# Three mask banks and one rank bank in the fuse stage, with the second rank piece of a row block issued behind the step's sums

## The chip, the cores and the metric

The kernel runs on one core of one Trainium2 chip. The metric is device time in microseconds (us); lower is better. The engines are TensorE (PE; its weight loads are listed as PEld), VectorE (DVE), ScalarE (ACT), GpSimd (POOL) and SyncE (SP), which issues the transfers. Each engine works through its own instructions in program order and waits on semaphores for the others. PE writes only into PSUM, whose eight banks of 128 x 512 fp32 are all in use in the stage that is changed.

## What is computed

Eight graphs of 1024 nodes with 128 features pass through four residual layers: an attention layer, a graph network on a thinned adjacency, a normalised-adjacency convolution and a max-degree layer. The second one is what matters here:

```python
def step(carry, n):                      # _dilate_pattern, one row after the other
    row = jnp.take(carry, n, axis=0)
    nbi = row.astype(jnp.int32)
    num = jnp.sum(nbi)
    sf = jnp.where(num > T_DIL, (num + K_DIL - 1) // K_DIL, 1)
    rank = jnp.cumsum(nbi)
    rm = row & (rank % sf == 0)
    ...
    keep = ~rm
    carry = carry.at[n].set(row & keep)
    carry = carry.at[:, n].set(carry[:, n] & keep)
...
adj_d = adj * keep
deg = jnp.clip(jnp.sum(adj_d, axis=-1, keepdims=True), 1.0, None)
agg = jnp.einsum('bij,bjd->bid', adj_d, x) / deg
out = agg @ Wr + x @ Wx + b
out = out / jnp.maximum(norm(out), NORM_EPS)
```

## The kernel before

The program is a row of stages: `attention_phase`, `removal_phase` (which settles how many entries each row loses), `fuse_phase`, two `layer_phase`s, `gcn_phase` and `maxdeg_phase`. The change lies in `fuse_phase` alone. It works on one graph `b` after the other, 0 to 7. For each graph it masks the transposed adjacency with the entries that were removed and adds up the first sage layer over it. At the same time it works out, for graph `b + 1`, which entries of each row were removed ("low").

A graph has eight row blocks of 128 rows, and the loop takes one block, a step `st`, at a time. What PE issues in a step, in this order:

- `masks(b, st, 0)` and `masks(b, st, 1)`: the two halves of the block's mask, 512 columns each, in one of the NM mask banks `pmask`. DVE's `masked_rows` (L1241) multiplies the adjacency by each half and then raises `masked`, which frees the bank. PE waits for this at L1060 before it writes mask number n, until mask n - NM is done.
- `ranks(b + 1, st)`: running counts along the rows of the next graph, in one of the NR rank banks `prank`. Blocks 0 to 3 have one piece of at most 512 columns, blocks 4 to 7 a first piece of 512 columns and a second one of 128 to 512, so a graph has 12 pieces. ACT's `distances` (L1162) reads each piece into a `dist` buffer in SBUF and raises `dist_ready`, which frees the bank. DVE's `removals` (L1229) compares it, which gives `low`, and frees the dist buffer. PE waits for `dist_ready` before it writes piece n, until piece n - NR has been read.
- side work in the one bank `misc`, by `misc_uses`: a product or a set of transposes in each step (`z` in step 0 and 7, `o2` in 1 and 2, `turn_r` in 3 and 4, `turn_h` in 5 and 6), which ACT, or DVE for `o2`, copies out before the next use.
- `sums(b, st - 1)`: eight fp32 products of the masked rows of the step before (L1113), added up in the three banks `acc`. `sums(b, 7)` comes behind step 7.

ACT works in each step through `distances(b + 1, st)` for all pieces of the block, then the side copy. Behind it come `squares(b - 1)` in step 0, `rectified(b - 1)` (L1190) in step 1, `norm_root` in step 2 and `norm_apply` (L122, eight instructions) in step 3. DVE works through `masked_rows(b, st)`, then `outputs(b - 1)` in step 0, `removals(b + 1, st)`, `projected` (L1247) for `o2` in steps 1 and 2, `weights` in step 1, `norm_mean` in step 2, `norm_scale` in step 3 and `batch_statistics` in step 6.

Ahead of the loop there is a prologue for graph 0: all its rank pieces, with `turn_h` and the first `z` between the first ones. PE may begin the masks of a graph once all 12 pieces of `low` for it are there (`low_ready`). Graph 7 has no next graph, so it runs without ranks.

Of the kernel before, what the change touches and what calls it, by code (L numbers as in the profile page):

```python
# [7 lines left out]
ACT = mybir.ActivationFunctionType  # L8
F32 = mybir.dt.float32
BF16 = mybir.dt.bfloat16  # L10
F16 = mybir.dt.float16
# [5 lines left out]
P = 128  # L17
HALF = 512
# [930 lines left out]
def fuse_phase(nc, z, A, K, scratch):  # L949

    B, N, NB, NH, HB, D = z.B, z.N, z.NB, z.NH, z.HB, z.D
    pieces = [(nb, hf * HALF, min((hf + 1) * HALF, (nb + 1) * P)) for nb in range(NB) for hf in range(NH)
              if hf * HALF < (nb + 1) * P]
    low0 = [sum((i + 1) * P for i in range(j)) for j in range(NB + 1)]
    NR, NM = 2, 2
    NC, CB = NB // 2, 2
    NP, NW = len(pieces), NB * NH
    ZW, AW = D + 1, 170
# [1 line left out]
    adjT = K["adj"]  # L960
    with Scope(nc, "fuse") as s:
        low = s.sb("low", [P, low0[NB]], BF16)
        dist = [s.sb(f"dist{i}", [P, HALF], F16) for i in range(NR)]
        h = K["h"]
        hT = s.sb("hT", [P, N], F32)
        zz = s.sb("z", [P, NB, ZW], F32)
# [5 lines left out]
        prank = [s.ps(f"prank{i}", [P, HALF]) for i in range(NR)]  # L972
# [15 lines left out]
        def of_block(nb):  # L988
            return [q for q in range(NP) if pieces[q][0] == nb]
# [22 lines left out]
        with nc.Block() as block:  # L1012
# [25 lines left out]
            @block.tensor  # L1038
            def _(pe):
                t = nc.tensor  # L1040

                def ranks(b, nb):

                    for q in of_block(nb):
                        _, lo, hi = pieces[q]
                        n = b * NP + q
                        if n >= NR:
                            pe.wait_ge(dist_ready, n - NR + 1)
                        first_jb, last_jb = lo // P, min(nb, (hi - 1) // P)
                        for jb in range(first_jb, last_jb + 1):  # L1050
                            a = max(jb * P, lo)
                            mm = t.matmul(prank[n % NR][:, a - lo:hi - lo], T8[:, b, jb, nb * P:(nb + 1) * P],  # L1052
                                          K["fore8"][:, a - jb * P:hi - jb * P], start=(jb == first_jb), stop=(jb == last_jb))
                        mm.then_inc(rank_ready, 1)

                def masks(b, pb, hf):

                    n = b * NW + pb * NH + hf
                    if n >= NM:
                        pe.wait_ge(masked, n - NM + 1)  # L1060
                    o = pmask[n % NM]
                    c0 = hf * HALF
                    own, up = (pb + 1) * P - c0, max(0, pb * P - c0)
                    if up < HALF:
                        t.matmul(o[:, up:HALF], K["minus8"][:], T8[:, b, pb, c0 + up:c0 + HALF], start=True, stop=False)
                    for c, k in ((0, min(HALF, up)), (up, P if 0 < own <= HALF else 0)):
                        if k > 0:
                            t.matmul(o[:, c:c + k], K["ident16"][:], low[:, low0[pb] + c0 + c:low0[pb] + c0 + c + k],
                                     start=(up >= HALF), stop=False)
                    for e in range(HB):  # L1070
                        qb = hf * HB + e
                        piece = o[:, e * P:(e + 1) * P]
                        if qb >= pb:
                            mm = t.matmul(piece, low[:, low0[qb] + pb * P:low0[qb] + (pb + 1) * P], K["ident16"][:],  # L1074
                                          start=False, stop=(e == HB - 1))
                        else:
                            mm = t.matmul(piece, T8[:, b, pb, qb * P:(qb + 1) * P], K["minus8"][:],
                                          start=False, stop=(e == HB - 1))
                    mm.then_inc(mask_ready, 1)

                def side_work(kind, b, half):

                    n = use_number[(kind, b, half)]
                    if n > 0:
                        pe.wait_ge(misc_free, n)
                    if kind == "turn_h":
                        if b > 0:
                            pe.wait_ge(h_ready, b)
                    elif kind == "turn_r":
                        pe.wait_ge(r_ready, b * 2 + half + 1)  # L1090
                    else:
                        pe.wait_ge(hT_ready, b * 2 + half + 1)
                    for e in range(HB):
                        ib = half * HB + e
                        if kind == "turn_h":
                            mm = t.transpose(miscv[:, e, :], h[:, ib, :], K["ident"][:])
                        elif kind == "turn_r":
                            mm = t.transpose(miscv[:, e, :], o[b % 2][:, ib, :], K["ident"][:])
                        else:
                            mm = t.matmul(miscv[:, e, :], hT[:, ib * P:(ib + 1) * P], K["Wr0" if kind == "z" else "Wx0"][:],  # L1100
                                          start=True, stop=True)
                    mm.then_inc(misc_ready, 1)

                def sums(b, jb):

                    if jb == 0 and b == 0:
                        pe.wait_ge(ones_ready, 1)
                    pe.wait_ge(z_ready, b * 2 + jb // HB + 1)
                    pe.wait_ge(masked, b * NW + (jb + 1) * NH)
                    for ib in range(NB):  # L1110
                        if jb == 0 and b > 0 and ib % 3 == 0:
                            pe.wait_ge(acc_free, 3 * (b - 1) + ib // 3 + 1)
                        mm = t.matmul(acc_tile(ib)[:, 0:ZW], adjT[b % 2][:, jb, ib * P:(ib + 1) * P], zz[:, jb, :],  # L1113
                                      start=(jb == 0 and ib % 3 == 0), stop=(jb == NB - 1), skip_group_check=True)
                    mm.then_inc(added, 1)
                    if jb == NB - 1:
                        pe.drain().then_inc(sums_ready, 1)

                ranks(0, 0)
                side_work("turn_h", 0, 0)  # L1120
                ranks(0, 1)
                side_work("turn_h", 0, 1)
                ranks(0, 2)
                ranks(0, 3)
                side_work("z", 0, 0)
                for nb in range(4, NB):
                    ranks(0, nb)
                for b in range(B + 1):
                    if b < B:
                        pe.wait_ge(low_ready, (b + 1) * NP)  # L1130
                    if b == B:
                        keep_busy(t, K, pmask[0][:], 26)
                    for st in range(NB):
                        if b < B:
                            for hf in range(NH):
                                masks(b, st, hf)
                            if b + 1 < B:
                                ranks(b + 1, st)
                        for use in misc_uses(b, st):
                            side_work(*use)  # L1140
                        if b < B and st > 0:
                            sums(b, st - 1)
                    if b < B:
                        sums(b, NB - 1)

            @block.scalar
            def _(act):
                a = nc.scalar
# [4 lines left out]
                def distances(b, nb):  # L1153
                    for q in of_block(nb):
                        _, lo, hi = pieces[q]
                        n = b * NP + q
                        act.wait_ge(rank_ready, n + 1)
                        if n >= NR:
                            act.wait_ge(dist_done, n - NR + 1)
                        tile = b * NB + nb  # L1160
                        bias = K["kb"][:, tile:tile + 1] if lo == 0 else K["kbhigh"][:, nb - NB // 2, b:b + 1]
                        a.activation(dist[n % NR][:, 0:hi - lo], prank[n % NR][:, 0:hi - lo], ACT.Abs, bias=bias)  # L1162
                        act.drain().then_inc(dist_ready, 1)  # L1163

                def side_copy(kind, b, half):
# [55 lines left out]
            def _(dve):  # L1221
                v = nc.vector

                def removals(b, nb):
                    for q in of_block(nb):
                        _, lo, hi = pieces[q]
                        n, tile = b * NP + q, b * NB + nb
                        dve.wait_ge(dist_ready, n + 1)
                        v.tensor_scalar(low[:, low0[nb] + lo:low0[nb] + hi], dist[n % NR][:, 0:hi - lo],  # L1229
                                        K["kd"][:, tile:tile + 1], None, ALU.is_equal).then_inc(low_ready, 1)  # L1230
                        dve.drain().then_inc(dist_done, 1)

# [893 lines left out]
```

## Time and profile before

| | |
|---|---|
| median of 3 runs | 1295.79 us (1294.36 to 1296.54) |
| profiled execution | 1293.96 us, span of its instructions 1292.2 us |
| PE, weight loads, DVE, ACT busy | 1156.5, 934.5, 780.2, 589.5 us |
| fuse stage | from 342.4 to about 643 us of the span |

The span runs from the first to the last instruction; the time of the execution also has what lies around it. Starts of rows in a timeline are counted from the start of the span. Matmuls are pipelined, so a row's length is longer than the distance to the next start. The distance between starts is therefore what a group of matmuls costs where nothing waits.

### The profile page before, as it was taken

To read this page: it belongs to the slowest core of one execution; us is meant where nothing else is said; L and a number is where in the kernel's file an instruction comes from. 1 tells how busy PE (TensorE), PEld (TensorE's weight loads), DVE (VectorE), ACT (ScalarE), POOL (GpSimd) and SP (SyncE) were. 2 spreads that over 40 slices of the span, in tenths; PEclk is the share of its full clock that TensorE was granted. 3 is DMA by queue.
4 is the path that set the end of the run, shared out by engine and by line. 5 is a ranking of instruction groups with operands and counts; after the bars stand their busy time and mean duration, and the time that the engine had idled before them with its cause. 6 is when DMAs were issued, how large, how long until landed. Compare 5 with 4: busy or idle time off the path is not lost. (4 is left out here: it accounts for less than half of the span.)

```text
span 1292.2 us, 27195 instructions
## 1 busy us (share of the span) xinstructions
PE 1156.5 (89%) x9833; PEld 934.5 (72%) x9833; DVE 780.2 (60%) x2899; ACT 589.5 (46%) x1533; POOL 114.7 (9%) x129
## 2 busy tenths in 40 slices
PE   4999698887598898898989999899999899997998
PEld 4999666664387777777879999699999655553554
DVE  5998577776556665656634453543536455545983
ACT  4888456566645544445222434413343443323441
POOL 3442000000000000000000000022323020110000
PEclk9999888876699999999989999999999899998999
DMA  8967012110335566555316575036757336543921
GB/s 327 327 262 284 11 24 34 23 27 14 135 129 231 228 250 240 225 190 205 133 49 260 230 281 224 22 123 232 289 208 303 131 131 256 218 177 128 407 68 49
DMA packets 105514, 228.93 MB, mean 177 GB/s; under 512 B 34528, under 2 KB 53152, under 8 KB 105376
## 3 DMA queue, kind: packets, MB, share of 16 engines
q1 hardware_dynamic: 104656, 227.07, 47.2%
q8 instruction: 81, 1.33, 0.4%
q14 instruction: 57, 0.47, 0.1%
q10 hardware_dynamic: 720, 0.07, 0.0%
HBM read 185.70 MB, written 37.75 MB: 173 GB/s over the span
## 5 line engine op out<-in xcount | busy, mean ns | idle before, releaser
L1431 PE MATMUL lay_acc<-lay_z,k_otheradj 128*128 128x128 f32 x1024 | 118.3, 277 | 0.0
L1431 PEld LDWEIGHTS lay_acc<-lay_z,k_otheradj 128*128 128x128 f32 x1024 | 117.1, 194 | 0.0
L1431 PE MATMUL lay_acc<-lay_z,k_keepadj 128*128 128x128 f32 x1024 | 117.0, 275 | 0.0
L1431 PEld LDWEIGHTS lay_acc<-lay_z,k_keepadj 128*128 128x128 f32 x1024 | 115.6, 192 | 0.0
L1479 ACT ACTIVATE lay_junk<-lay_o 128x128 bf16<-128x128 f32 x128 | 37.8, 296 | 124.7 <-DVEq L1568 124.5
L1545 DVE TENSOR_TENSOR lay_o<-lay_ring,k_vec 128x512 f32<-128x512 f32 x32 | 22.1, 692 | 108.1 <-PE lay_ring L1424 108.1
L1525 POOL TENSOR_TENSOR lay_bl<-k_vec,k_mask 128x256 f32<-128x256 f32 x32 | 21.2, 663 | 607.1 <-DVEq L1558 603.4
L333 PE MATMUL att_acc<-att_rhs,att_adjT 128*128 128x130 f32 x512 | 60.0, 281 | 13.3 <-POOLq L285 12.3
L333 PEld LDWEIGHTS att_acc<-att_rhs,att_adjT 128*128 128x128 f32 x512 | 59.3, 196 | 13.9 <-POOLq L285 12.4
L1162 ACT ACTIVATE fuse_dist<-fuse_prank,k_kb 128x512 f16<-128x512 f32 (+2 forms) x64 | 38.4, 600 | 60.7 <-PE fuse_prank L1052 59.3
L1113 PE MATMUL fuse_acc<-fuse_z,k_otheradj 128*128 128x129 f32 x512 | 63.5, 277 | 0.9 <-DVEq L1263 0.8
L1487 ACT ACTIVATE lay_o<-lay_o,lay_nrm 128x128 f32<-128x128 f32 x128 | 39.4, 389 | 54.2 <-DVE lay_nrm L1579 54.2
L1113 PE MATMUL fuse_acc<-fuse_z,k_keepadj 128*128 128x129 f32 x512 | 63.1, 277 | 0.8 <-DVEq L1263 0.8
L1241 DVE SCALAR_TENSOR_TENSOR k_otheradj<-fuse_pmask,k_otheradj 128x512 f32<-128x512 f32 x64 | 44.1, 689 | 28.9 <-PE fuse_pmask L1074 16.4
L1113 PEld LDWEIGHTS fuse_acc<-fuse_z,k_otheradj 128*128 128x128 f32 x512 | 59.9, 192 | 2.0 <-DVEq L1263 1.6
L1113 PEld LDWEIGHTS fuse_acc<-fuse_z,k_keepadj 128*128 128x128 f32 x512 | 59.8, 192 | 1.7 <-DVEq L1263 1.2
L1229 DVE TENSOR_SCALAR fuse_low<-fuse_dist,k_kd 128x512 bf16<-128x512 f16 (+2 forms) x96 | 30.7, 320 | 49.7 <-ACTq L1163 44.8
L333 PE MATMUL att_acc<-att_rhs,k_keepadj 128*128 128x130 f32 x512 | 58.1, 276 | 1.8 <-DVEq L441 0.9
L333 PEld LDWEIGHTS att_acc<-att_rhs,k_keepadj 128*128 128x128 f32 x512 | 57.5, 191 | 2.4 <-issue 2.4
L1052 PE MATMUL fuse_prank<-k_fore,k_T 128*128 128x128 fp8e5 (+3 forms) x288 | 46.7, 290 | 13.2 <-PEq L140 7.6
L1241 DVE SCALAR_TENSOR_TENSOR k_keepadj<-fuse_pmask,k_keepadj 128x512 f32<-128x512 f32 x64 | 44.1, 689 | 23.9 <-PE fuse_pmask L1074 14.1
L1689 PE MATMUL gcn_agg<-k_keepadj,gcn_hs 128*128 128x512 f32 x128 | 56.4, 593 | 1.2 <-DVE k_keepadj L1786 1.2
(293 smaller groups left out, 2592.7 us busy)
## 6 DMA issues: line engine op xcount, KB each, us to landing
k_keepadj<-in_adj_cols SPq DMA_DIRECT2D x28, 1024.0 KB, 9.3
k_keepadj<-keptT SPq DMA_DIRECT2D x12, 2048.0 KB, 11.1
k_otheradj<-keptT SPq DMA_DIRECT2D x12, 2048.0 KB, 11.0
att_adjT<-in_adj_cols SPq DMA_DIRECT2D x16, 1024.0 KB, 7.9
k_otheradj<-in_adj_cols SPq DMA_DIRECT2D x16, 1024.0 KB, 9.6
keptT<-k_keepadj SPq DMA_DIRECT2D x16, 1024.0 KB, 4.8
keptT<-k_otheradj SPq DMA_DIRECT2D x16, 1024.0 KB, 4.9
lay_rowf<-in_adj_rows SPq DMA_DIRECT2D x32, 512.0 KB, 14.6
```

The source lines that it names most:

```text
L333: mm = t.matmul(acc[n % NA][:, e // 2, e % 2, 0:W], adjT[i % 2][:, jb, ib * P:(ib + 1) * P], rhs[i % 2][:, jb, 0:W], start=(jb == 0), stop ...
L1052: mm = t.matmul(prank[n % NR][:, a - lo:hi - lo], T8[:, b, jb, nb * P:(nb + 1) * P], K["fore8"][:, a - jb * P:hi - jb * P], start=(jb == f ...
L1113: mm = t.matmul(acc_tile(ib)[:, 0:ZW], adjT[b % 2][:, jb, ib * P:(ib + 1) * P], zz[:, jb, :], start=(jb == 0 and ib % 3 == 0), stop=(jb == ...
L1162: a.activation(dist[n % NR][:, 0:hi - lo], prank[n % NR][:, 0:hi - lo], ACT.Abs, bias=bias)
L1229: v.tensor_scalar(low[:, low0[nb] + lo:low0[nb] + hi], dist[n % NR][:, 0:hi - lo], K["kd"][:, tile:tile + 1], None, ALU.is_equal).then_inc ...
L1241: v.scalar_tensor_tensor(rows, pmask[n % NM][:], -0.5, rows, ALU.is_lt, ALU.mult)
L1431: mm = t.matmul(acc[i % 2][k][:, ib % HB, :], adjT[i % 2][:, jb, ib * P:(ib + 1) * P], zz[i % 2][:, jb, :], start=(jb == 0), stop=(jb == N ...
L1479: a.activation(junk[:, ib, :], o[i % 2][:, ib, :], ACT.Square, accum_out=nrm[:, 0, ib:ib + 1])
L1487: last = a.activation(o[i % 2][:, ib, :], o[i % 2][:, ib, :], ACT.Relu, scale=nrm[:, 4, ib:ib + 1])
L1525: g.tensor_tensor(bl[:], along_tiles(K["vec"][:, V_BL, :], 2), along_features(K["mask"][:, tile:tile + 2], D), ALU.mult)
L1545: v.tensor_tensor(o[i % 2][:, half * HB:(half + 1) * HB, :], ring[n % NS][:], along_tiles(K["vec"][:, V_B1 + layer, :], HB), ALU.add)
L1689: mm = t.matmul(agg[b % 2][:, sl], hs[b % 2][:, jb, :], adjT[b % 2][:, jb, sl], start=(jb == 0), stop=(jb == NB - 1))
```

## The change

One PSUM bank goes from the ranks to the masks: NR is 1 instead of 2, and NM is 3 instead of 2. The two SBUF buffers `dist` stay two, under a number of their own, ND. PE's `ranks` takes a number `half` and issues one piece at a time. In the loop the second piece of a block goes behind `sums(b, st - 1)`. In the prologue the two pieces stay next to each other. The orders of ACT and DVE stay as they are.

```diff
-    NR, NM = 2, 2
+    NR, ND, NM = 1, 2, 3
...
-        dist = [s.sb(f"dist{i}", [P, HALF], F16) for i in range(NR)]
+        dist = [s.sb(f"dist{i}", [P, HALF], F16) for i in range(ND)]
...
-                def ranks(b, nb):
+                def ranks(b, nb, half):
 
-                    for q in of_block(nb):
+                    for q in of_block(nb)[half:half + 1]:
                         _, lo, hi = pieces[q]
                         n = b * NP + q
                         if n >= NR:
...
                 for nb in range(4, NB):
-                    ranks(0, nb)
+                    ranks(0, nb, 0)
+                    ranks(0, nb, 1)
                 for b in range(B + 1):
...
                             if b + 1 < B:
-                                ranks(b + 1, st)
+                                ranks(b + 1, st, 0)
                         for use in misc_uses(b, st):
                             side_work(*use)
                         if b < B and st > 0:
                             sums(b, st - 1)
+                        if b + 1 < B:
+                            ranks(b + 1, st, 1)
...
-                        if n >= NR:
-                            act.wait_ge(dist_done, n - NR + 1)
+                        if n >= ND:
+                            act.wait_ge(dist_done, n - ND + 1)
...
-                        a.activation(dist[n % NR][:, 0:hi - lo], prank[n % NR][:, 0:hi - lo], ACT.Abs, bias=bias)
+                        a.activation(dist[n % ND][:, 0:hi - lo], prank[n % NR][:, 0:hi - lo], ACT.Abs, bias=bias)
```

The first place is PE in step 4 and the head of step 5 of the second graph, b = 1; later graphs but the last read alike. The names in brackets are semaphores under the name that they had first in the program: `att_chunk_loaded1_1` is `dist_ready` here, `att_mask_loaded` is `masked`, `att_set1` is `misc_free`. Before:

```order
L1052 MATMUL fuse_prank0<-k_fore8,k_T8 128x128
L1052 MATMUL fuse_prank1<-k_fore8,k_T8 128x128 [waits att_chunk_loaded1_1]
L1098 MATMUL fuse_misc<-k_ident,fuse_o0 128x128 [waits att_sums_ready,att_set1]
L1098 MATMUL fuse_misc<-k_ident,fuse_o0 128x128 x3
L1113 MATMUL fuse_acc<-fuse_z,k_otheradj 128x129 [waits att_mask_loaded,att_mask_ready]
L1113 MATMUL fuse_acc<-fuse_z,k_otheradj 128x129 x7
L1068 MATMUL fuse_pmask0<-fuse_low,k_ident16 128x512 [waits att_mask_loaded]
L1077 MATMUL fuse_pmask0<-k_minus8,k_T8 128x128 x4
L1065 MATMUL fuse_pmask1<-k_T8,k_minus8 128x384 [waits att_mask_loaded]
```

The same place on PE in the changed kernel:

```order
L1052 MATMUL fuse_prank0<-k_fore8,k_T8 128x128
L1098 MATMUL fuse_misc<-k_ident,fuse_o0 128x128 [waits att_sums_ready,att_set1]
L1098 MATMUL fuse_misc<-k_ident,fuse_o0 128x128 x3
L1113 MATMUL fuse_acc<-fuse_z,k_otheradj 128x129 [waits att_mask_loaded,att_mask_ready]
L1113 MATMUL fuse_acc<-fuse_z,k_otheradj 128x129 x7
L1052 MATMUL fuse_prank0<-k_fore8,k_T8 128x128 [waits att_chunk_loaded1_1]
L1068 MATMUL fuse_pmask2<-fuse_low,k_ident16 128x512 [waits att_mask_loaded]
L1077 MATMUL fuse_pmask2<-k_minus8,k_T8 128x128 x4
L1065 MATMUL fuse_pmask0<-k_T8,k_minus8 128x384 [waits att_mask_loaded]
```

The second piece of block 4, one matmul of 128 columns, moved from ahead of the transposes and the sums to behind them, and directly ahead of the masks of step 5. It writes the bank of the first piece and so waits for its reader.

The second place is PE in the prologue, the pieces of blocks 4 and 5 of graph 0. Before:

```order
L1052 MATMUL fuse_prank0<-k_fore8,k_T8 128x512 [waits att_chunk_loaded1_1]
L1052 MATMUL fuse_prank0<-k_fore8,k_T8 128x384
L1052 MATMUL fuse_prank0<-k_fore8,k_T8 128x256
L1052 MATMUL fuse_prank0<-k_fore8,k_T8 128x128
L1052 MATMUL fuse_prank1<-k_fore8,k_T8 128x128 [waits att_chunk_loaded1_1]
L1052 MATMUL fuse_prank0<-k_fore8,k_T8 128x512 [waits att_chunk_loaded1_1]
```

The same rows on PE in the changed kernel:

```order
L1052 MATMUL fuse_prank0<-k_fore8,k_T8 128x512 [waits att_chunk_loaded1_1]
L1052 MATMUL fuse_prank0<-k_fore8,k_T8 128x384
L1052 MATMUL fuse_prank0<-k_fore8,k_T8 128x256
L1052 MATMUL fuse_prank0<-k_fore8,k_T8 128x128
L1052 MATMUL fuse_prank0<-k_fore8,k_T8 128x128 [waits att_chunk_loaded1_1]
L1052 MATMUL fuse_prank0<-k_fore8,k_T8 128x512 [waits att_chunk_loaded1_1]
```

No instruction moved here. Each piece now goes to the same bank, so each wait is for the piece just ahead instead of the one before that.

## Rows read from the trace of the kernel before

**Rows 1.** Stretches: start:end, length, busy time (instructions) by engine, PE's granted clock.
```profile
301.00:349.00 48.00, 30.14 (x344) 19.59 (x345) 31.02 (x197) 31.39 (x74) 0.12 (x1) 0.50 0.17 52
349.00:356.20 7.20, 3.97 (x26) 1.85 (x24) 2.58 (x8) 5.37 (x9) 0.00 (x0) 1.00 0.75 304
649.34:652.75 3.41, 1.28 (x8) 0.84 (x8) 1.03 (x2) 2.26 (x7) 0.00 (x0) 0.98 0.01 2
652.75:659.58 6.83, 5.60 (x16) 2.52 (x16) 2.40 (x7) 0.29 (x1) 0.00 (x0) 0.51 0.62 229
```

**Rows 2.** Waits of PE, 342 to 645 us: total us, times, longest.
```profile
PE fuse_pmask L1065 <- DVEq L1242: 6.0, 14, 0.7
PE fuse_prank L1052 <- ACTq L1163: 5.6, 10, 0.9
PE fuse_pmask L1068 <- DVEq L1242: 3.7, 6, 0.6
```

**Rows 3.** Timeline of graph 3, steps 2 to 4: start, length, instructions, idle before.
```profile
471.21 0.28 PE L1065 MATMUL fuse_pmask<-k_T,k_minus 128*128 128x256 fp8e5 x1 [0.67 <-DVEq L1242]
...
473.26 1.16 PE L1100 MATMUL fuse_misc<-k_Wx,fuse_hT 128*128 128x128 f32 x8 [0.30 <-DVEq L1248]
...
481.27 0.39 PE L1068 MATMUL fuse_pmask<-fuse_low,k_ident 128*128 128x512 bf16 x1 [0.62 <-DVEq L1242]
...
483.19 3.19 ACT L122 ACTIVATE k_h<-k_X,fuse_n_stat 128x128 f32<-128x128 f32 x8 [0.82 <-DVE fuse_n_stat L105]
...
486.28 0.67 ACT L1162 ACTIVATE fuse_dist<-fuse_prank,k_kb 128x512 f16<-128x512 f32 x1
```

**Rows 4.** The same timeline of graph 3, steps 5 and 6, PE.
```profile
487.02 0.88 PE L1052 MATMUL fuse_prank<-k_fore,k_T 128*128 128x512 fp8e5 x6 [0.51 <-ACTq L1163]
488.26 0.66 PE L1096 MATMUL fuse_misc<-k_ident,k_h 128*128 128x128 f32 x4 [0.36 <-ACTq L1177]
...
490.54 0.38 PE L1068 MATMUL fuse_pmask<-fuse_low,k_ident 128*128 128x512 bf16 x1
...
491.48 1.03 PE L1052 MATMUL fuse_prank<-k_fore,k_T 128*128 128x512 fp8e5 x7
492.35 0.61 PE L1096 MATMUL fuse_misc<-k_ident,k_h 128*128 128x128 f32 x4
```

**Rows 5.** Timeline of the prologue, 345 to 356 us.
```profile
345.15 1.91 PE L1052 MATMUL fuse_prank<-k_fore,k_T 128*128 128x384 fp8e5 x7
346.17 0.58 ACT L1162 ACTIVATE fuse_dist<-fuse_prank,k_kb 128x384 f16<-128x384 f32 x1 [0.17 <-PE fuse_prank L1052]
...
349.68 0.69 ACT L1162 ACTIVATE fuse_dist<-fuse_prank,k_kb 128x512 f16<-128x512 f32 x1 [0.17 <-PE fuse_prank L1052]
350.44 0.88 PE L1052 MATMUL fuse_prank<-k_fore,k_T 128*128 128x512 fp8e5 x6 [0.92 <-ACTq L1163]
...
355.14 0.69 ACT L1162 ACTIVATE fuse_dist<-fuse_prank,k_kbhigh 128x512 f16<-128x512 f32 x1 [0.16 <-PE fuse_prank L1052]
...
356.30 0.39 PE L1065 MATMUL fuse_pmask<-k_T,k_minus 128*128 128x512 fp8e5 x1 [1.36 <-DVE fuse_low L1229]
```

**Rows 6.** Timeline of graph 0: pieces of one and four matmuls and their readers.
```profile
357.24 0.22 PE L1052 MATMUL fuse_prank<-k_fore,k_T 128*128 128x128 fp8e5 x1
...
357.50 0.37 ACT L1162 ACTIVATE fuse_dist<-fuse_prank,k_kb 128x128 f16<-128x128 f32 x1 [1.67 <-PE fuse_prank L1052]
...
382.37 1.25 PE L1052 MATMUL fuse_prank<-k_fore,k_T 128*128 128x512 fp8e5 x8
383.12 0.69 ACT L1162 ACTIVATE fuse_dist<-fuse_prank,k_kb 128x512 f16<-128x512 f32 x1 [1.92 <-PE fuse_prank L1052]
```

**Rows 7.** Timeline of graph 0, step 5 and the head of step 6, PE.
```profile
374.45 0.88 PE L1052 MATMUL fuse_prank<-k_fore,k_T 128*128 128x512 fp8e5 x6 [0.58 <-ACTq L1163]
...
377.40 0.38 PE L1068 MATMUL fuse_pmask<-fuse_low,k_ident 128*128 128x512 bf16 x1
```

**Rows 8.** The page's costliest groups, DVE's masks: busy us, mean ns, idle before.
```profile
L1241 DVE SCALAR_TENSOR_TENSOR k_otheradj<-fuse_pmask,k_otheradj 128x512 f32<-128x512 f32 x64 | 44.1, 689 | 28.9 <-PE fuse_pmask L1074 16.4
```

More of the change, by code:

```diff
@@ L1117, in sums @@
                         pe.drain().then_inc(sums_ready, 1)
-                ranks(0, 0)
+                ranks(0, 0, 0)
                 side_work("turn_h", 0, 0)
-                ranks(0, 1)
+                ranks(0, 1, 0)
                 side_work("turn_h", 0, 1)
-                ranks(0, 2)
-                ranks(0, 3)
+                ranks(0, 2, 0)
+                ranks(0, 3, 0)
                 side_work("z", 0, 0)
                 for nb in range(4, NB):
-                    ranks(0, nb)
+                    ranks(0, nb, 0)
+                    ranks(0, nb, 1)
                 for b in range(B + 1):
@@ L1228, in removals @@
                         dve.wait_ge(dist_ready, n + 1)
-                        v.tensor_scalar(low[:, low0[nb] + lo:low0[nb] + hi], dist[n % NR][:, 0:hi - lo],
+                        v.tensor_scalar(low[:, low0[nb] + lo:low0[nb] + hi], dist[n % ND][:, 0:hi - lo],
                                         K["kd"][:, tile:tile + 1], None, ALU.is_equal).then_inc(low_ready, 1)
```

## The prediction

> **What bounds the kernel now.** I read the page first, for which engine sets the pace in the fuse stage. Then came PE's waits in that stage, the stretches with PE's granted clock, and the timelines of the prologue, of graph 0 and of graph 3. The other middle graphs repeat graph 3 to within some tenths.
>
> PE waits for a free mask bank for 6.0 + 3.7 = 9.7 us in all, and for the reader of a rank bank for 5.6 us [rows 2]. The first is what a third mask bank can take away, the second is what a single rank bank can add to. Whether the 9.7 us are worth anything has to be read from what PE waits for next.
>
> In graph 3 that is plain. PE waits 0.67 us for a mask bank at 471.21. Two groups later it waits again, until 473.26, for `misc`, which DVE has to clear (`projected`) [rows 3]. DVE is then behind with `outputs`, masks, `removals` and `projected` of the two steps, and none of these waits for a mask that PE is late with. At 481.27 PE waits for a mask bank again. The last link of this chain is ACT's `norm_apply`, 3.19 us from 483.19 on, started by DVE's `norm_scale`. Behind it ACT reads the first piece of block 4 at 486.28, and at 487.02 PE may write on [rows 3, 4]. So from the start of a graph to 487.02 DVE and ACT set the pace. From 487.02 to the end of the graph it is PE: one short wait at 488.26 [rows 4], then none. So steps 5 to 7 decide: a graph costs what PE still has to do behind that wait for ACT.
>
> **The mask banks.** With three banks, mask n waits for mask n - 3. The waits at 471.21 and 481.27 go or shrink (the second half of step 4 still needs the first half of step 3). At the first place PE comes to `misc` up to 1 us early and waits there until 473.26 all the same. At the second place PE is about 0.8 us early, and comes early to the next reader, ACT behind `norm_apply`, whose end hangs on DVE alone. I take a gain of nothing per graph. If the cover were gone, the gain would be the 9.7 us, which is the other bound.
>
> **The moved piece, graphs 1 to 6.** In step 4 PE now issues piece one of block 4, the transposes, the sums, and then piece two, a single matmul. It writes the only rank bank, so it needs ACT's read of piece one, from 486.28 to 486.95. The row of the release is 0.07 us later, at 487.02 [rows 3, 4]. That time does not move. Before, the masks of step 5 were issued ahead of this wait; now they are behind it. What PE does from 487.02 to the masks of step 6:
> - before: six rank matmuls, a wait, transposes and sums, up to 490.54, which is 3.52 us [rows 4];
> - after: one rank matmul and the restart 0.10; masks of step 5 0.94 (490.54 to 491.48); first piece of block 5, four matmuls, 0.55; transposes 0.44 and sums 1.79; second piece of block 5, two matmuls, 0.16. That is 3.98 us. The 0.55 is the 0.87 us of seven matmuls (491.48 to 492.35), shared by columns: 1280 of 2048. The 0.44 and 1.79 are the 2.28 us from 488.26 to 490.54, less 0.05 for the restart. The wait for `misc` at 488.26 is gone, since ACT has copied it during the masks.
>
> That is +0.46 us a graph. In step 7 one more wait opens. ACT must read the second piece of block 6 (384 columns, 0.58 us as in the prologue [rows 5]), which PE issues only behind the sums of step 6, and copies `misc` behind it, which takes as long. It ends about 5.6 us after the head of step 6, and PE is there after 5.5 us. With the restart I take 0.14 us. Sum +0.6 us, six graphs: +3.6 us.
>
> **Graph 0.** It has no `outputs` and no `turn_r`, so nothing waits for `misc` there. PE goes from 374.45 to the masks of step 6 in 377.40 - 374.45 = 2.95 us [rows 7]. The same list as above now gives 3.98: +1.03, with the wait of step 7 +1.2 us. Graph 7 has no ranks; its mask waits lie ahead of `misc` waits: 0.
>
> **Prologue.** Here the two pieces stay together and the banks were all that let PE write one piece while ACT read the other. With one bank they take turns. A full piece costs 0.75 us from its first matmul to ACT's start (382.37 to 383.12), 0.69 us of ACT and 0.07 us back to PE (350.37 to 350.44): 1.51 us [rows 5, 6]. A piece of one matmul costs 0.26 + 0.37 + 0.07 = 0.70 us (357.24 to 357.50, then ACT) [rows 6]. Those of 256 and 384 columns lie between; by columns I take 0.9 and 1.2 us. The last one, of block 7, is a full one. Behind the first piece of block 4 follow 0.70 + 1.51 + 0.9 + 1.51 + 1.2 + 1.51 + 1.50 = 8.8 us. Before, from ACT's end of that piece (349.68 + 0.69 = 350.37) to its end of the last (355.14 + 0.69 = 355.83) it was 5.46 us [rows 5]. That is +3.35 us. Ahead of it the piece of block 3 now waits for ACT's read of block 2, which ends at 346.17 + 0.58 = 346.75, so PE writes from 346.82 instead of 345.15 + 0.64 (768 columns at 1.2 GHz) = 345.79. PE runs at half clock there [rows 1], and part of the delay is won back as the clock rises at 349: +0.7 us. Together +4.0 us, up to the first mask, which stands at 356.30 now. Bounds: 3.3 us without the part ahead, and 8.8 - 5.46 + 1.03 = 4.4 us with all of it.
>
> **Nothing else moves.** DVE comes to the masks of steps 6 to 8 later, since `removals` of the second piece stands ahead of them in its order. Its two masks of a step take 0.69 us each [rows 8], and two `removals` are shorter; PE needs 3.98 us for a step. By my count the last piece of `low` is there 0.7 us ahead of the first mask that needs it. Were that slack gone, each graph would pay the shortfall.
>
> **Sum.** +3.6 + 1.2 + 4.0 = +8.8 us on the profiled execution's 1293.96 us: 1302.8 us. The median of the runs stands 1.8 us above that execution, so +8.8 on 1295.79 gives 1304.6 us.
>
> **Rivals.**
> - *PE's clock falls in the prologue.* Up to 349 us, in the removal stage and the head of the prologue, the granted clock is 0.50, with PE busy 30.14 of 48 us; from 349 on it is 1.00, with 3.97 busy of 7.2 us. At 649.34 PE is busy for 1.28 of 3.41 us, and the next stretch is at 0.51 [rows 1]. With one bank PE is busy for about 4 of some 10.5 us, between these. If the clock is at its lower level while it counts ranks, blocks 4 to 7 of graph 0 (7680 columns) take 3.2 us more, and the first masks about 1 us: +8.8 + 4 gives 1308.8. The Trainium skill, "TensorE: Matmul & The Clock Gate", section "A second HAM failure mode: psum-queue depth-cycling", says that a kernel which cycles through PSUM banks can idle PE so often between groups that the clock goes back and forth. By that rule the clock would fall here too. For it speaks 649.34, against it that 55% busy did not lower it in the stretch from 349. 0.25.
> - *The moved piece is free, only the prologue pays.* If ACT's read of block 4 came before PE is through with the sums of step 3 (PE is there at about 485, ACT at 487), the masks would not be held: +4.0, 1299.8. The rows speak against it by 2 us. 0.10.
> - *The mask waits are real (the other side).* If DVE is late because PE is late with masks, taking away 9.7 us of waits also pulls in `misc` and `norm_apply`. Then 9.7 - 4.0 for the prologue - 0.5 for the rest gives 5 us less, 1291. It decides if at least 4 us of the 9.7 reach `norm_apply`. Against it: DVE has nothing of these steps to wait for from PE while PE waits for `misc` at 473.26 [rows 3]. 0.08.
> - *It all cancels.* Half of the mask waits come back, 1296 or so. 0.07.
>
> **How the numbers follow.** The forecast has 0.50: 1304.6, its own range 1302 to 1306.5. Of the others I keep the clock and the free piece within reach and leave out the two on the low side: 1299.3 to 1309.5 us. No change here means within 0.2%, 2.6 us, which is also about what the measurement can tell. Faster 0.08, same 0.08 (the cancelling case and a little), slower 0.84.
>
> **What the profile would show.** Right: the first mask of graph 0 near 360.3 instead of 356.3; middle graphs longer by 0.6 us; no waits of PE for masks at L1065 and L1068 worth naming, but waits of 2 us a graph at L1052 for ACT; the wait for `misc` in step 2 grown by what the masks lost. Wrong: a shorter distance from a graph's first mask to its `norm_apply` (then the mask banks were the bound), waits on `low` at a graph's first mask, waits of the sums of step 7 for DVE, or a clock below 1.00 behind 349 us.

## The result and the profile after

The changed kernel takes 1315.98 us (median of 4 runs, 1315.18 to 1317.22) against 1296.16 us before (1294.36 to 1296.79). The ratio is 1.0156 with a 95% interval of 1.0138 to 1.0174: 1.6% slower, about 20 us. Slower was forecast, with 8.8 us; the forecast of 1304.6 us and its range up to 1309.5 us are both too low. Its profiled execution has a span of 1314.7 us, 22.5 us more than before.

PE's waits from 342 to 670 us, as in [rows 2]:

```profile
PE fuse_prank L1052 <- ACTq L1166: 20.7, 17, 2.1
PE fuse_misc L1100 <- DVEq L1251: 6.3, 7, 1.2
PE fuse_misc L1098 <- DVEq L1251: 3.0, 6, 0.5
PE fuse_pmask L1065 <- DVEq L1245: 2.1, 12, 0.2
```

And the wait for `misc` at L1100 before:

```profile
PE fuse_misc L1100 <- DVEq L1248: 2.1, 7, 0.4
```

The mask waits fell from 9.7 to 2.1 us. The wait for `misc` at L1100 and the waits for ACT at L1052 took their place; the latter stood at 5.6 us before [rows 2].

Stretches of the changed kernel: start:end, length, then busy time by engine (PE first), then PE's granted clock ahead of the last two figures. The first is the prologue, the next two are graph 0, then come graph 1, graph 2, a part of graph 1, and graph 7:

```profile
344.31:365.67 21.36, 13.92 (x53) 7.16 (x53) 3.85 (x12) 8.97 (x16) 0.11 (x1) 0.50 0.51 196
365.67:371.03 5.36, 5.36 (x31) 4.30 (x32) 2.09 (x4) 0.97 (x2) 0.00 (x0) 0.50 0.01 3
371.03:401.78 30.75, 28.83 (x270) 25.81 (x268) 16.66 (x45) 11.66 (x23) 0.00 (x0) 1.00 0.38 142
401.78:441.68 39.90, 35.52 (x307) 30.40 (x308) 23.71 (x67) 19.01 (x53) 0.00 (x0) 0.96 0.52 202
441.68:480.27 38.59, 33.97 (x307) 29.02 (x307) 23.70 (x67) 19.00 (x53) 0.00 (x0) 1.00 0.58 219
425.64:429.05 3.41, 3.41 (x22) 2.93 (x20) 1.90 (x4) 1.24 (x2) 0.00 (x0) 0.54 0.19 76
637.27:665.25 27.98, 26.61 (x255) 24.32 (x255) 17.41 (x38) 7.20 (x29) 0.00 (x0) 1.00 0.36 143
```

Where the 22.5 us of the span are, by the starts of the stage and of each graph's first mask:

| part | before | after | difference | forecast |
|---|---|---|---|---|
| ahead of the fuse stage | 342.36 | 344.31 | +1.95 | 0 |
| prologue | 13.94 | 21.36 | +7.42 | +4.0 |
| graph 0 | 32.10 | 36.11 | +4.01 | +1.2 |
| graphs 1 to 6 | 226.71 | 235.49 | +8.78 | +3.6 |
| graph 7 and all behind it | 677.09 | 677.43 | +0.34 | 0 |

The first line isn't the change's: kernels below that are alike up to that point begin the stage anywhere from 342.69 to 345.02 us.

The clock is the new thing in these rows. It stays at 0.50 for the whole prologue and the first 5.36 us of graph 0, where before it was 1.00 from 349 us on [rows 1]. Then it falls again for 3.4 us in graphs 1, 3 and 5, which take 39.90, 39.87 and 40.23 us. Graphs 2, 4 and 6 between them take 38.59, 38.59 and 38.31.

The prologue with one bank, at the lower clock, on PE and ACT:

```profile
356.52 0.50 PE L1052 MATMUL fuse_prank<-k_fore,k_T 128*128 128x256 fp8e5 x2 [0.80 <-ACTq L1166]
357.06 0.47 ACT L1165 ACTIVATE fuse_dist<-fuse_prank,k_kbhigh 128x256 f16<-128x256 f32 x1 [0.62 <-PE fuse_prank L1052]
...
357.61 1.25 PE L1052 MATMUL fuse_prank<-k_fore,k_T 128*128 128x512 fp8e5 x4 [0.59 <-ACTq L1166]
358.89 0.69 ACT L1165 ACTIVATE fuse_dist<-fuse_prank,k_kb 128x512 f16<-128x512 f32 x1 [1.36 <-PE fuse_prank L1052]
```

PE and ACT take turns, as forecast: ACT waits 1.36 us for PE, then PE waits for ACT. A full piece takes 1.28 us from PE's start to ACT's, where it was 0.75 at the higher clock [rows 6]. The clock comes up only 5.36 us into the masks, where PE no longer waits.

### The profile page after: what moved, and what is told of

Same layout as the page of the kernel before. It is cut to its first block and busy times, and to the rows that moved or that the text cites. A ratio compares the mean times of both kernels' runs of the same rounds, so it can differ in the third digit from the quotient of the medians.

```text
span 1314.7 us, 27195 instructions
## 1 busy us (share of the span) xinstructions
PE 1170.5 (89%) x9833; PEld 943.2 (72%) x9833; DVE 779.1 (59%) x2899; ACT 589.2 (45%) x1533; POOL 114.7 (9%) x129
## 5 line engine op out<-in xcount | busy, mean ns | idle before, releaser
L1052 PE MATMUL fuse_prank<-k_fore,k_T 128*128 128x128 fp8e5 (+3 forms) x288 | 56.8, 311 | 28.7 <-ACTq L1166 20.7
L1113 PE MATMUL fuse_acc<-fuse_z,k_otheradj 128*128 128x129 f32 x512 | 66.3, 283 | 0.9 <-DVEq L1266 0.8
L1113 PEld LDWEIGHTS fuse_acc<-fuse_z,k_otheradj 128*128 128x128 f32 x512 | 62.6, 198 | 2.0 <-DVEq L1266 1.6
L1052 PEld LDWEIGHTS fuse_prank<-k_fore,k_T 128*128 128x128 fp8e5 x288 | 26.8, 104 | 47.0 <-ACTq L1166 26.4
L1692 PE MATMUL gcn_agg<-k_otheradj,gcn_hs 128*128 128x512 f32 x128 | 56.3, 592 | 0.0
## 6 DMA issues: line engine op xcount, KB each, us to landing
k_otheradj<-in_adj_cols SPq DMA_DIRECT2D x16, 1024.0 KB, 10.2
```

The costliest lines, as they stand in the source:

```text
L1692: mm = t.matmul(agg[b % 2][:, sl], hs[b % 2][:, jb, :], adjT[b % 2][:, jb, sl], start=(jb == 0), stop=(jb == NB - 1))
```

## The experiments

Each was timed beside the kernel before. Intervals are those of the ratio to it. In each diff the lines with + are the experiment's.

**a1_borrow: the prologue without the turns.** For graph 0 the pieces with an odd number go into the third mask bank, which no mask uses yet. Both the matmuls and ACT's read then use `rank_bank(n)`.

```diff
+        def rank_bank(n):
+            return pmask[NM - 1] if n < NP and n % 2 else prank[0]
...
+                        lag = 2 if n < NP else NR
-                        if n >= NR:
-                            pe.wait_ge(dist_ready, n - NR + 1)
+                        if n >= lag:
+                            pe.wait_ge(dist_ready, n - lag + 1)
```

> The changed kernel, but graph 0's rank pieces in the prologue take turns between the rank bank and the third mask bank, which nothing uses yet. Theory (the prologue's turns and the low clock that they keep cost most of the loss): prologue from its first matmul to the first mask back at 13.9 us (21.4 in the changed kernel), granted clock 1.00 before the first mask, graph 0 at 33.3 us (36.1), so 7.4 + 2.8 = 10.2 us less than the changed kernel, about 1305.8 us. Rival (the loss lies in the loop): the prologue shrinks by 4.0 us only and the clock stays at its lower level into graph 0, about 1312 us.

Measured: 1306.4 us, ratio 1.0088 (1.0071 to 1.0105).

```profile
344.76:358.70 13.94, 10.28 (x52) 6.64 (x53) 3.84 (x12) 8.96 (x16) 0.11 (x1) 0.76 0.77 301
358.70:392.01 33.31, 31.39 (x296) 28.05 (x299) 18.74 (x48) 12.61 (x25) 0.00 (x0) 1.00 0.35 130
392.01:431.90 39.89, 35.40 (x305) 30.51 (x308) 23.73 (x67) 18.99 (x53) 0.00 (x0) 0.96 0.52 203
```

These stretches are prologue, graph 0 and graph 1. The prologue is back at 13.94 us to the hundredth, the clock is up before the first mask, and graph 0 takes 33.31 us. The theory's numbers hold: one bank in the prologue cost 10.2 us in all. Graph 0 is now the forecast's own, +1.21 over 32.10, and so are its parts: about 3.9 us from ACT's release to the masks of step 6, where it was 2.95 [rows 7], and 0.2 us more behind them. The graphs behind it are unchanged, the slow ones too.

**a4_busy_prologue: the turns stay, PE is kept busy.** `keep_busy` issues matmuls of 512 columns whose result nobody reads; its last argument is how many.

```diff
                 for nb in range(4, NB):
                     ranks(0, nb, 0)
+                    keep_busy(t, K, pmask[0][:], 2)
                     ranks(0, nb, 1)
+                    keep_busy(t, K, pmask[0][:], 2)
```

> The changed kernel with two unused matmuls of 512 columns behind each rank piece of blocks 4 to 7 in the prologue, into a mask bank that is not yet in use; they lie in PE's waits for ScalarE. Theory (half of the loss up to graph 0 is the clock, which stays low because PE idles): the granted clock rises before the first mask, the prologue takes 18 to 19 us instead of 21.4, graph 0 33.3 instead of 36.1, together 5 to 6 us less than the changed kernel, about 1310.5 us. Rival (the clock has nothing to do with it; the turns between PE and ScalarE alone do it): the added matmuls lengthen the prologue or change nothing, 1316 us or more.

Measured: 1307.0 us, ratio 1.0084 (1.0067 to 1.0101), with 16 matmuls more, in eight groups of two.

```profile
342.87:352.50 9.63, 8.36 (x34) 5.39 (x35) 1.47 (x5) 4.79 (x9) 0.11 (x1) 0.50 0.89 343
352.50:361.63 9.13, 6.84 (x37) 2.49 (x35) 2.37 (x8) 4.17 (x7) 0.00 (x0) 0.98 0.25 99
361.63:394.95 33.32, 31.39 (x296) 28.05 (x299) 18.74 (x48) 12.62 (x25) 0.00 (x0) 1.00 0.34 127
```

The clock comes up just behind 352.5 us. The prologue takes 9.63 + 9.13 = 18.76 us and graph 0 33.32. That is 2.6 and 2.8 us less than in the changed kernel, won by work that computes nothing. So the clock is a cause of its own, apart from the turns. The rest of the 8.4 us between the two spans is graph 1, at 38.26 us without a fall of the clock, and a stage that begins 1.4 us earlier. The expected 1310.5 us did not have the first of these. The four executions lie from 1303.15 to 1308.13 us, so the 9.0 us between the medians are less sure than the 5.4 us read from these rows.

**a2_two_masks: without the third mask bank.**

```diff
-    NR, ND, NM = 1, 2, 3
+    NR, ND, NM = 1, 2, 2
```

> The changed kernel with two mask banks instead of three, one bank unused; one rank bank and the moved piece stay. Theory (the third mask bank is worth nothing, its waits come back as waits for misc and ScalarE): within 1.5 us of the changed kernel, 1314.5 to 1317.5 us, with mask waits of some 8 us back in the table of waits and the misc waits smaller. Rival (the mask waits are real and the third bank hides part of the loss): slower than the changed kernel by up to 9.7 us, about 1325 us.

Measured: 1310.25 us, ratio 1.0118 (1.0101 to 1.0135). This is neither: 5.7 us faster than with the third bank. The mask waits are back, at 6.0 us at L1065 and 5.1 at L1077, of which 1.3 are missing records, as shown below. Graphs 1 to 6 take 38.25, 38.60, 38.23, 38.58, 38.57 and 38.31 us. The even ones are as in the changed kernel to 0.01 us, the odd ones 1.65 us shorter, and from 371 us to the end of graph 7 the clock is never below 1.00. PE around step 4 of graph 1, with two mask banks:

```profile
419.31 0.39 PE L1077 MATMUL fuse_pmask<-k_minus,k_T 128*128 128x128 fp8e5 x4 [0.84 <-DVEq L1245]
419.90 0.39 PE L1065 MATMUL fuse_pmask<-k_T,k_minus 128*128 128x512 fp8e5 x1 [0.20 <-DVEq L1245]
...
424.84 0.23 PE L1052 MATMUL fuse_prank<-k_fore,k_T 128*128 128x128 fp8e5 x1 [1.50 <-ACTq L1166]
```

And in the changed kernel, with three:

```profile
418.32 0.38 PE L1068 MATMUL fuse_pmask<-fuse_low,k_ident 128*128 128x512 bf16 x1
418.54 0.39 PE L1077 MATMUL fuse_pmask<-k_minus,k_T 128*128 128x128 fp8e5 x4
...
420.77 1.95 PE L1113 MATMUL fuse_acc<-fuse_z,k_otheradj 128*128 128x129 f32 x16
424.86 0.23 PE L1052 MATMUL fuse_prank<-k_fore,k_T 128*128 128x128 fp8e5 x1 [2.13 <-ACTq L1166]
...
427.70 2.74 PE L1113 MATMUL fuse_acc<-fuse_z,k_otheradj 128*128 128x129 f32 x16
```

PE is released at 424.84 and 424.86, so the bank moved nothing. What it did is draw the idle time together: the wait ahead of the masks went, and 1.50 us ahead of the rank piece became 2.13. The wait that went is 0.62 us, as before [rows 3]: of the 0.84 in the row, 0.22 are the matmul of L1068, whose record is missing in that trace. So 0.62 and 1.50 us in two pieces stand against 2.13 us in one. The graph begins at the same time in both, 401.76 and 401.78 us. Behind the single wait the clock falls in graphs 1, 3 and 5, and the sums take 2.74 us instead of 1.95.

**c1_fill_loop: the same three banks, the idle time filled.** On top of a1_borrow:

```diff
                         if b + 1 < B:
+                            if st == 4:
+                                n = b * NW + 5 * NH
+                                pe.wait_ge(masked, n - NM + 1)
+                                keep_busy(t, K, pmask[n % NM][:], 7)
                             ranks(b + 1, st, 1)
```

> The prologue with the borrowed bank (a1_borrow), and in step 4 of each graph seven unused matmuls of 512 columns ahead of the moved rank piece, into the mask bank that step 5 writes next; they lie in the 2.13 us in which PE waits there for ScalarE. Theory (PE's idle time, drawn together at one place by the third mask bank, lets the granted clock fall in every second graph): no stretch below 1.00 between the first mask of graph 0 and graph 7, graphs 1, 3 and 5 at 38.3 us instead of 39.9, 4.5 to 5 us less than a1_borrow, about 1301.5 us. Rival (the long graphs come from something else, DMA traffic or a wait): 1306.4 us or more, the added matmuls only in the way.

Measured: 1297.71 us, ratio 1.0022 (1.0012 to 1.0032).

```profile
412.32 1.67 PE L1323 MATMUL fuse_pmask<-k_fore,k_ident 128*128 128x512 fp8e5 x7
414.61 0.23 PE L1056 MATMUL fuse_prank<-k_fore,k_T 128*128 128x128 fp8e5 x1 [0.62 <-ACTq L1174]
```

These are the filler and the rest of the wait in graph 1. The stretches are graph 1 and graph 2:

```profile
391.54:429.77 38.23, 35.37 (x313) 29.63 (x314) 23.70 (x67) 18.99 (x53) 0.00 (x0) 1.00 0.54 212
429.77:468.36 38.59, 35.48 (x314) 29.64 (x315) 23.69 (x67) 19.00 (x53) 0.00 (x0) 1.00 0.57 219
```

Graph 1 takes 38.23 us instead of 39.89, graph 2 is unchanged at 38.59, and the clock is 1.00 in both. The three graphs give back 5.0 us as expected. Another 1.8 us of the spans lie behind the start of graph 7, 675.7 against 677.5 us: there the clock is low for 3.4 instead of 6.8 us as the next stage begins. The expected 1301.5 us had no such part, and the median lies 3.8 us below it.

**a3_move_only: the moved piece with two and two banks.**

```diff
-    NR, ND, NM = 1, 2, 3
+    NR, ND, NM = 2, 2, 2
```

> Two rank and two mask banks as before, with only the second piece of a block moved behind the sums. Theory (the move costs nothing by itself; it costs through the single bank, which puts the masks of step 5 behind ScalarE's read): 1294 to 1298 us, with a wait of PE for ScalarE in step 5 as before and none ahead of the moved piece. Rival (issuing the piece late is itself what costs, since ScalarE copies misc only behind it): each of seven graphs 0.5 to 1 us longer, 1300 us or more.

Measured: 1294.57 us, ratio 0.9997 (0.9988 to 1.0007). The time is the theory's, the stage is not: graphs 1 to 6 take 228.95 us, 0.37 us each more than before. PE on step 5 of graph 1 shows a part of it:

```profile
414.44 0.72 PE L1052 MATMUL fuse_prank<-k_fore,k_T 128*128 128x512 fp8e5 x4 [0.50 <-ACTq L1166]
...
415.67 0.66 PE L1096 MATMUL fuse_misc<-k_ident,k_h 128*128 128x128 f32 x4 [0.52 <-ACTq L1180]
```

The wait for `misc` is 0.52 us, where it was 0.36 [rows 4], but not because ACT copies later: from the release to the transposes it is 415.67 - 414.44 = 1.23 us, and it was 1.24 (487.02 to 488.26). The two matmuls of block 5's second piece no longer lie in that wait. They come behind the sums and add their own 0.16 us. The other 0.22 us lie in steps 6 and 7, as in the changed kernel (below); there ACT copies `misc` behind the late piece, as the rival says, but the wait that shows for it in step 7 is about 0.1 us. So issuing the piece late does cost, a third of a microsecond a graph, only in small part by the rival's way. It doesn't reach the time, because from graph 7 to the end this profiled execution takes 674.8 us against 677.1, again with 3.4 instead of 6.8 us of low clock behind the stage.

**b2_unmoved: one rank bank, three mask banks, both pieces together.**

```diff
                             if b + 1 < B:
                                 ranks(b + 1, st, 0)
+                                ranks(b + 1, st, 1)
...
-                        if b + 1 < B:
-                            ranks(b + 1, st, 1)
```

> The changed kernel with the second piece of a block put back directly behind the first, so one rank bank and three mask banks without the move. Theory (with a single rank bank PE stands still between two pieces for ScalarE's whole read, 0.69 us and the way there and back, in steps 5 to 7, and in step 4 ahead of transposes and sums as well, 2.2 us more): a graph 4 to 5 us longer than in the changed kernel, 1340 to 1350 us. Rival (the move is what costs): not slower than the changed kernel, 1316 us or less.

Measured: 1356.52 us, ratio 1.0484 (1.0458 to 1.051). Graphs 1 to 6 take 44.81 to 46.44 us. Steps 4 and 5 of graph 1:

```profile
427.71 0.29 PE L1052 MATMUL fuse_prank<-k_fore,k_T 128*128 128x128 fp8e5 x1 [4.54 <-ACTq L1165]
...
434.11 0.34 PE L1052 MATMUL fuse_prank<-k_fore,k_T 128*128 128x256 fp8e5 x2 [0.80 <-ACTq L1165]
```

PE waits 4.54 us for ACT in step 4 and 0.80 us in each of steps 5 to 7, and the clock falls for 3.4 or 6.8 us in each of these graphs behind the long wait. The direction is the theory's. The size is above it, most likely by these falls of the clock; no run took them away here. The move is thus what makes a single rank bank bearable; it is the bank that costs.

**b3_split_before: the chain itself.** The kernel before, with ACT's `norm_apply` in two halves, the second behind the reads of step 4; the first `turn_h` waits for the first half only.

```diff
-                            pe.wait_ge(h_ready, b)
+                            pe.wait_ge(h_ready, 2 * b - 1 + half)
...
+                def norm_half(b, half):
+                    if half == 0:
+                        act.wait_ge(w["scale_ready"], b + 1)
...
-                        if b + 1 < B and st == 3:
-                            norm_apply(nc, act, x_tile(b + 1), h[:], w, b, h_ready)
+                        if b + 1 < B and st in (3, 4):
+                            norm_half(b, st - 3)
```

> The kernel before (two and two banks, nothing moved), with ScalarE's norm_apply split: four of its eight instructions in step 3, four behind the distances of step 4; the first turn_h waits for the first four only. Theory (from a graph's start to step 5 the chain through norm_apply is the limit, and PE's wait at L1052 is its end): the wait of 0.5 us at L1052 and the wait for misc behind it go, 1.1 us a graph, 7 graphs, about 1288 us. Rival (another wait takes its place, on h_ready or on misc): within 2 us of before.

Measured: 1285.38 us, ratio 0.993 (0.9908 to 0.9951), faster than both kernels. ACT in steps 3 and 4 of graph 3:

```profile
481.05 1.65 ACT L1198 ACTIVATE k_h<-k_X,fuse_n_stat 128x128 f32<-128x128 f32 x4 [0.82 <-DVE fuse_n_stat L105]
482.61 0.67 ACT L1162 ACTIVATE fuse_dist<-fuse_prank,k_kb 128x512 f16<-128x512 f32 x1
...
484.62 1.65 ACT L1198 ACTIVATE k_h<-k_X,fuse_n_stat 128x128 f32<-128x128 f32 x4
```

ACT reads the first piece of block 4 1.56 us behind the start of `norm_apply`, where it was 3.09 us (483.19 to 486.28, [rows 3]). Graphs 1 to 6 take 36.3 to 36.7 us, 1.2 to 1.3 us less each. Of the 10 us between the medians some 1.7 are not the split's: behind the start of graph 7 this execution takes 675.4 us against 677.1, with the shorter low stretch. The 9.7 us of mask waits are all still there, at 6.0 and 3.7.

**b4_split_borrow: both together.** The changed kernel with the borrowed bank and the split of b3.

> The changed kernel with the borrowed bank in the prologue and norm_apply split as in b3_split_before. Theory (norm_apply is what holds the moved piece, 2.13 us a graph; without it the third mask bank can show its gain, and no idle time is left at one place for the clock to fall): graphs of 36 to 36.8 us, all at clock 1.00, in all 1288 us or a little less. Rival (the single rank bank finds another wait, in steps 5 to 7, behind ScalarE that now works there): graphs above 37.5 us, slower than before.

Measured: 1288.53 us, ratio 0.9954 (0.994 to 0.9968). Graphs 1 to 6 take 36.7 to 37.05 us, all at clock 1.00, and PE waits 0.59 us ahead of the moved piece:

```profile
410.77 0.23 PE L1056 MATMUL fuse_prank<-k_fore,k_T 128*128 128x128 fp8e5 x1 [0.59 <-ACTq L1170]
```

The theory is right on the clock. The gain that it gave the third mask bank isn't there: most graphs are 0.36 us longer than with two and two banks and nothing moved in b3, about what the move alone cost in a3.

## Why the prediction was wrong

The step that failed is the clock. The sum put PE's clock at 1.00 from 349 us on, in the prologue, in graph 0 and in every graph behind it. It was 0.50 until 5.36 us into graph 0 and fell again in graphs 1, 3 and 5. Its other terms held where the clock is 1.00.

- *The mask banks give nothing*: right. In graph 2 it takes 465.10 - 441.68 = 23.42 us from the first mask to the release by ACT; before it was 449.44 - 426.01 = 23.43 (rows below). The mask waits came back at `misc` (L1100, 2.1 to 6.3 us) and ahead of the rank piece. The rival on the other side, 5 us faster, falls with it.
- *The moved piece*: right. From the release to the masks of step 6 the profile has 465.10 to 469.04, 3.94 us, against 3.98 in the sum. In steps 6 to 8 graph 2 takes 11.23 us (469.04 to 480.27), where a graph before took 11.00 or 11.01; the wait of step 7 was put at 0.14 and is about 0.2. Graphs 1 to 6 cost 3.8 us without the falls of the clock (8.78 less three times 1.65); the sum said 3.6. a3 splits this: about 0.37 us a graph come with the move alone, the rest with the single bank.
- *Graph 0*: +1.21 us in a1_borrow, where the sum had +1.2.
- *Prologue*: the turns were right, at the wrong clock. The sum let the clock rise at 349 us as before. It took 7.4 us instead of 4.0. With filler, and the clock up at 352.5, it is 4.8; the 4.0 at a clock of 1.00 from 349 on were never measured.
- *The clock in the prologue*: the part that a rival had. "PE's clock falls in the prologue" had 0.25 and a price of 4 us. It happened, and cost 6.2 us up to the end of graph 0: 2.8 in graph 0, measured by a1 and a4, and 3.4 in the prologue, which is 7.4 less the forecast 4.0. Its price counted the ranks of blocks 4 to 7 and about 1 us of masks. But the clock stayed low for 5.36 us of masks and sums, where PE is the limit and each matmul counts. The weighing leaned on the 3.97 us busy of 7.2 from 349 on as a sign that the clock bears such idling; with one bank PE idles more, and it was low already and had to rise.
- *What wasn't in any case*: that removing mask waits could lower the clock inside the loop. That is 3 times 1.65, 5.0 us, shown by a2 (two mask banks, no falls) and by c1 (three, but filled). The section of the Trainium skill that the prediction cites, "A second HAM failure mode: psum-queue depth-cycling" in "TensorE: Matmul & The Clock Gate", warns of idling between groups. The traces agree that idle time in PE's stream can lower the clock, but not that its amount decides: waits of 0.62, 0.20 and 1.50 us (a2) kept it at 1.00 in all six graphs, the single one of 2.13 us lost it in three of six.

Together 9.0 us of the mechanism (4.0, 1.2 and 3.8, the first as forecast) and 11.2 us of clock (3.4, 2.8 and 5.0) make 20.2 us, the three middle lines of the table. The other 2.3 us of the spans lie ahead of the stage and behind it. That the 20.2 come so near to the 19.8 us between the medians is luck: the two profiled executions lie 22.8 us apart.

The rows of graph 2 for the first two points, before and then changed:

```profile
426.01 0.38 PE L1065 MATMUL fuse_pmask<-k_T,k_minus 128*128 128x512 fp8e5 x1 [0.26 <-issue]
...
449.44 0.88 PE L1052 MATMUL fuse_prank<-k_fore,k_T 128*128 128x512 fp8e5 x6 [0.50 <-ACTq L1163]
```

```profile
465.10 0.23 PE L1052 MATMUL fuse_prank<-k_fore,k_T 128*128 128x128 fp8e5 x1 [2.12 <-ACTq L1166]
...
469.04 0.38 PE L1068 MATMUL fuse_pmask<-fuse_low,k_ident 128*128 128x512 bf16 x1
```

Open: why graphs 1, 3 and 5 lose the clock and 2, 4 and 6, with the same wait of 2.13 us, keep it. In a4_busy_prologue it is graphs 3 and 5 alone: its graph 1 has the same instructions and the same wait as in the changed kernel, begins 6.8 us earlier, and keeps the clock. So more than the wait decides, and when it falls may be a part of it. No run varied the position of the wait by itself.

## What to carry to other kernels

Before a buffer is moved from one ring to another, ask of each wait in the table what the engine meets next. A wait that another wait covers is worth nothing, and a ring of one makes writer and reader take turns. When PE's waits are redistributed, price the clock as well, with every matmul that would run at the lower level: here a single gap cost more than the same idle time in pieces. And a wait for a reader may be shortened at the reader: splitting the eight instructions ahead of it gave 0.7% (some 0.1% of it the low stretch named below), where the third mask bank gave nothing.

## What the runs showed that was not expected

- Work that computes nothing made the kernel faster twice: 16 matmuls in the prologue by 9.0 us of the median (a4_busy_prologue against the changed kernel), of which 5.4 us are up to the end of graph 0; and 7 in each of seven graphs by 8.7 us (c1_fill_loop against a1_borrow), of which 5.0 us are the three graphs.
- The low stretch as the next stage begins is 3.4 us in some kernels (a2, a3, c1, b3 and b4) and 6.8 us in others (before, after, a1 and a4). From the start of graph 7 to the end the first take 674.8 to 676.0 us and the others 677.1 to 677.5, with the same code in the stages behind; b2, with 6.8 us, stands between them at 676.4. Differences of 0.2% between such kernels may be nothing more.
